# A decoder block on one core: the middle stage gives its last batch to the cross attention, whose maxima then go through one pair of PSUM banks

## The reference

```python
nx = _ln(x, ln1_scale, ln1_bias)
q, k, v = heads(nx @ W_qkv)                       # (4, 16, 1024, 16)
x = x + merge(attend(q, k, v, causal)) @ W_self_out
nx = _ln(x, ln2_scale, ln2_bias)
q = heads(nx @ W_q); k, v = heads(ctx_1024 @ W_kv)   # 154 keys
x = x + merge(attend(q, k, v, None)) @ W_cross_out
nx = _ln(x, ln3_scale, ln3_bias)
return x + relu(nx @ W1 + b1) @ W2 + b2
```

## Time and profile before

| | us |
|---|---|
| median of 3 runs | 997.35 (996.07 to 999.2) |
| profiled execution | 995.61, its span 993.9 |
| TensorE busy | 962.8 (97%) |
| DVE busy | 740.0 (74%) |
| ACT busy | 638.0 (64%) |
| POOL busy | 256.7 (26%) |
| DMA traffic | 124 MB, 38% of the 16 engines' time |

### The profile page before, as it was taken

How to read it: one execution, slowest core, us unless ns; L and a number is a source line. 1 busy time by engine, 2 the same in 40 slices (tenths; PEclk the granted TensorE clock), 3 DMA queues, 4 the chain that set the end, 5 groups by cost and what they waited for, 6 DMA issues and landing times.

```text
span 993.9 us, 20076 instructions
## 1 busy us (share of the span) xinstructions
PE 962.8 (97%) x7632; PEld 605.5 (61%) x7632; DVE 740.0 (74%) x1175; ACT 638.0 (64%) x1371; POOL 256.7 (26%) x451
## 2 busy tenths in 40 slices
PE   4999999999999999999999998999999999999998
PEld 3877664555555555555543764444444699999997
DVE  7578879999999999999923776888887744455542
ACT  4653357777777777777777324788887644444443
POOL 6521122333322222232244110111115212222210
PEclk9999999999999999999999998999999999999999
DMA  7996762222323131313525887244441112221001
GB/s 211 315 349 231 249 193 79 84 93 67 110 66 109 55 102 51 107 51 101 172 85 172 266 318 233 83 136 136 147 129 35 63 45 64 64 65 63 23 23 43
DMA packets 78272, 124.01 MB, mean 125 GB/s; under 512 B 10624, under 2 KB 51872, under 8 KB 73120
## 3 DMA queue, kind: packets, MB, share of 16 engines
q1 hardware_dynamic: 78176, 122.73, 37.8%
HBM read 72.48 MB, written 49.17 MB: 122 GB/s over the span
## 4 chain that ended last, share of the span: by engine, by line
PE 86%; DVE 9%; DMA 2%; issue 1%; ACT 1%; SPq 1%; POOL 0%; ACTq 0%; DVEq 0%
PE bank L862 20%; PE bank L841 18%; PE bank L717 11%; PE bank L698 10%; PE bank L699 9%; PE bank L700 9%; DVE mx L1222 6%; PE bank L725 2%; PE bank L896 2%; PE bank L690 2%; PE bank L685 2%; PE bank L738 1%; DMA qx_parts<-probs 1%; DVE nx_mem L1208 1%; DMA q_st<-qx_parts 1%
## 5 line engine op out<-in xcount | busy, mean ns | idle before, releaser
L1115 ACT ACTIVATE probs<-bank 128x512 f32<-128x512 f32 (+3 forms) x1024 | 455.1, 524 | 122.1 <-PE bank L841 117.2
L1222 DVE TENSOR_REDUCE mx<-bank 128x2 f32<-128x1024 f32 (+5 forms) x416 | 433.6, 1082 | 39.1 <-PE bank L717 27.3
L841 PE MATMUL bank<-q_st,k_st 64*128 64x512 f32 (+3 forms) x1024 | 287.6, 428 | 6.4 <-ACT probs L1115 3.3
L841 PEld LDWEIGHTS bank<-q_st,k_st 64*128 64x128 f32 x1024 | 135.8, 185 | 181.3 <-ACT probs L1115 165.4
L862 PE MATMUL bank<-probs,nx_mem 128*32 128x512 f32 (+3 forms) x2048 | 231.6, 529 | 0.4 <-POOL probs L1583 0.4
L717 PE MATMUL bank<-k_st,q_st 62*128 62x154 f32 (+4 forms) x1280 | 225.7, 348 | 4.9 <-DVE mx L1222 2.6
L717 PEld LDWEIGHTS bank<-k_st,q_st 62*128 62x128 f32 x1280 | 143.5, 187 | 49.2 <-DVE mx L1222 30.5
L1583 POOL TENSOR_SCALAR_AFFINE_SELECT probs<-probs 128x256 f32<-128x256 f32 x256 | 103.9, 407 | 204.8 <-ACT probs L1115 204.2
L1592 POOL TENSOR_TENSOR oN<-oT,rs 128x256 f32<-128x256 f32 x64 | 40.5, 633 | 213.3 <-DVE rs L1326 213.3
L1153 ACT ACTIVATE hT<-bank,b_sb 128x512 f32<-128x512 f32 x64 | 44.2, 690 | 73.0 <-PE bank L700 73.0
L1474 DVE TENSOR_TENSOR hT_lo<-hT,hT_hi 128x512 fp32r<-128x512 f32 x64 | 42.6, 686 | 54.5 <-ACT hT_hi L1156 53.5
(11 more groups left out here) (126 smaller groups left out, 1276.2 us busy)
## 6 DMA issues: line engine op xcount, KB each, us to landing
q_st<-q_parts SPq DMA_DIRECT2D x48, 256.0 KB
q_st<-qx_parts SPq DMA_DIRECT2D x48, 256.0 KB
xt<-in_x_dram SPq DMA_DIRECT2D x16, 512.0 KB, 5.7
q_parts<-probs SPq DMA_DIRECT2D x16, 512.0 KB, 4.3
k_parts<-probs SPq DMA_DIRECT2D x16, 512.0 KB, 4.3
k_st<-k_parts SPq DMA_DIRECT2D x32, 256.0 KB
qx_parts<-probs SPq DMA_DIRECT2D x16, 512.0 KB, 6.3
v_aug<-vst_mem SPq DMA_DIRECT2D x8, 544.0 KB, 4.5
```

Of the source, the lines that this page charges most:

```text
L841: pe.matmul(bank[:, score_bank(a, use), 0:n], keys_of(a, v0)[rows, i // 2, P * kb:P * kb + P], q_st[w][rows, i // 2, lo:lo + n], start=Tru ...
L1115: act.activation(probs[:, use % NPT, 0:n], bank[:, score_bank(a, use), 0:n], ACT.Exp, scale=SCALE).then_inc(a.exp_done, 1)
L1222: dve.tensor_reduce(mx[:, par, part].rearrange("p (j y) -> p j y", j=2)[:, :, blocks.start:blocks[-1] + 1:blocks.step], banks[:, :, 0:len( ...
```

## The change

The last batch (n = 6 and 7) leaves the middle stage. Its two halves are worked off in spans 0 to 8 of cross attention (`late_c` on TensorE, ACT and DVE, `first_e` on SyncE): projection in steps 1 and 2 of a half, transposes in step 10, query products in steps 13 and 14, where a half has 16 steps, that is four spans. They use banks 6 and 7, so the maxima of cross attention have the pair (2, 3) alone from the first tile of span 0 until the turn of span 8 (`RING_X`, `ring_of`). The tiles of units 0 and 1 move to n = 3, 4 and 5. Normalized tokens and product parts of the late batch lie in memory that is free by then (`nx_late`, `parts_late`). SyncE waits for the stored parts of a batch ahead of the loads of its first unit, and loads and stores of the last batch move. For the last two units the ring of score banks begins with the usual ones. In self attention the slots of tiles and sums change. The final stage's first transposes come one step later. The diff, cut to its core:

```diff
         SA = Attention("S", True, L, L // P, q_parts, k_parts, v_aug, self_ctx, [0, 1, 2], [3], [(4, 5), (6, 7)],
-                       units_at=(1, 7, 7, 13, 13, 17, 21, 23, 28, 30, 34, 34, 38, 38, 44, 45, 47, 49, 52, 54), turn_at=2,
-                       weigh_at=(4, 0, 1, 1, 2, 1, 1, 1, 1, 1, 0, 2),
+                       units_at=(1, 7, 7, 13, 13, 18, 22, 24, 29, 30, 34, 34, 37, 40, 43, 43, 46, 49, 53, 53), turn_at=2,
+                       weigh_at=(4, 0, 1, 1, 3, 2, 2, 2, 1, 1, 0, 2),
...
-        EARLY_X = {3: (3,), 4: (1, 3), 5: (1, 3), 6: (0, 1, 2, 3), 7: (0, 1, 2)}
-        LATE_X = 6
+        NC, HALF_STEPS = 2 * B - 2, 16
+        EARLY_X = {3: (3,), 4: (0, 1, 2, 3, 3), 5: (0, 1, 1, 2, 3, 3)}
+        LATE_X = 4
...
-        def ring_x(n):
-            return 1 if n < LATE_X else 2
+        RING_X = (sum(n < LATE_X for n, _ in places_x), 2 * XA.MT + 1, (XA.MT + 1) * (2 * HALF_STEPS // XA.NS + 2) - XA.M0 + 2)
+        def ring_of(a, use):
+            return 1 if a is XA and (use < RING_X[0] or RING_X[1] <= use < RING_X[2]) else 2
...
-            return [y, *(a.s_banks[(use - at + c) % a.SB] for c in range(a.SB)), x][at % END_RING[a]]
+            return [*(a.s_banks[(use - at + c) % a.SB] for c in range(a.SB)), y, x][at % END_RING[a]]
...
@@ SyncE
+                        if a is XA and (v0 + 3) % 4 == 0:
+                            for s in range(4):
+                                sp.wait_ge(C.parts_stored[s], 16 + 16 * ((v0 + 3) // 4 + 1))
                         load_stacks(a, v0 + 3, b, "qk" if a.causal else "q")
...
-            sums_c(2, 0, True)
+            sums_c(2, 0, False)
...
             for hf in range(2):
-                sums_c(3, hf, False)
-                products_c(2, hf)
-                if hf:
-                    keys_x(3)
-                    load_stacks(XA, 2, 0, "q")
-            products_c(3, 0)
+                load_dense(C, x, self_ctx, 3, hf)
+            products_c(2, 0)
+            keys_x(3)
+            load_stacks(XA, 2, 0, "q")
             rows(XA, 0, 0)
-            products_c(3, 1)
             sp.wait_ge(v_spare, 2)
             load_values(XA, 1, 0)
+            products_c(2, 1)
             load_stacks(XA, 3, 0, "q")
...
             def first_e(w):
+                hf, part = divmod(w, HALF_STEPS // XA.NS)
+                if hf < 2 and part == 2:
+                    sums_c(B - 1, hf, False)
+                if 0 < hf < 3 and part == 0:
+                    products_c(B - 1, hf - 1)
...
@@ TensorE
-                    if use == 4 * a.NS * (4 * B - 2):
+                    if use == 4 * a.NS * (4 * B - 2) + a.SB:
                         pe.wait_ge(a.m_free, (a.MT + 1) * 4 * B - 1)
...
+            def late_c(hf, r):
+                n = NC + hf
+                if hf > 1:
+                    return
+                if r in (1, 2):
+                    if hf:
+                        pe.wait_ge(C.lo_ready, 2 + 2 * (n - 1) + r)
+                    elif r == 1:
+                        pe.wait_ge(XA.m_free, RING_X[1])
+                    project_c(B - 1, hf, r - 1, o_bank=6)
+                if r == 10:
+                    transposes(C, n, hf, 6, nx_late)
+                if r in (13, 14):
+                    c = r - 13
+                    pe.wait_ge(C.nxT_ready, 2 * n + 2)
+                    project(bank[:, 6 + c], wqx_sb, slice(P * c, P * c + P), nxT[:, hf]).then_inc(C.p_ready, 1)
...
-                if step == 4:
+                if step == 5:
                     transposes(E, 0, 0, 2)
...
@@ ACT
+                if r == 11:
+                    scaled(C, 1, n, hf, 6)
+                if r in (14, 15):
+                    c = r - 14
+                    if hf:
+                        act.wait_ge(C.parts_stored[c], 16 + 16 * B)
+                    high(C, 2 * n + c, late_part(n, c)[:, 0, :], bank[:, 6 + c, :])
...
@@ DVE, called in window(v0) ahead of each tile n
+            def late_c(hf, w, n):
+                x = NC + hf
+                if w == 0 and n == 0 and 0 < hf < 3:
+                    low(C, 2 * (x - 1) + 1, late_part(x - 1, 1), bank[:, 7, :])
+                if hf > 1:
+                    return
+                if w == 1 and n in (0, 2):
+                    if n == 0:
+                        dve.wait_ge(x1_stored[hf], 16 * (B - 1) + 16)
+                    residual(C, B - 1, hf, n // 2, 6, 32)
+                if w == 1 and n == 3:
+                    moments(C, xn, x, hf)
+                if w == 2 and n == 1:
...
+                    normalize(C, xn, x, hf, nx_late)
+                if w == 3 and n == XA.MT:
+                    low(C, 2 * x, late_part(x, 0), bank[:, 6, :])
```

More of the change, by code:

```diff
@@ L679, in _, with transposes @@
         def _(pe):
-            def transposes(ph, n, hf, b0):
+            def transposes(ph, n, hf, b0, src=None):
                 pe.wait_ge(ph.nx_ready, n + 1)
+                src = nx[:, hf] if src is None else src
                 for k in range(KC):
                     for t in range(TT):
-                        last = pe.transpose(bank[:, b0 + k, P * t:P * t + P], nx[:, hf, t, P * k:P * k + P], ident[:, :])
+                        last = pe.transpose(bank[:, b0 + k, P * t:P * t + P], src[:, t, P * k:P * k + P], ident[:, :])
                     last.then_inc(ph.tp_ready, 1)
@@ L701, in product, with max_tile @@
                 return last
-            def max_tile(a, v0, b, n, ring):
+            def max_tile(a, v0, b, n):
                 v, w = v0 + 4 * b, v0 % 4
                 blocks, k0, keys, _ = a.tiles[n]
-                use, banks = a.tile_use(v, n), unit_banks(a, a.tile_use(v0, n), ring)
+                use, banks = a.tile_use(v, n), unit_banks(a, a.tile_use(v0, n))
+                ring = ring_of(a, use)
+                if a is XA and use == RING_X[2]:
+                    pe.wait_ge(C.lo_ready, 2 + 2 * 2 * B)
                 if n == 0:
@@ L895, in project_c @@
                     for k in range(KC):
-                        last = pe.matmul(bank[:, 4 + i, D * t:D * t + D], cT[:, hf, k, P * (2 * i + t):P * (2 * i + t) + P],
+                        last = pe.matmul(bank[:, o_bank + i, D * t:D * t + D], cT[:, hf, k, P * (2 * i + t):P * (2 * i + t) + P],
                                          wso_sb[:, k, :], start=(k == 0), stop=(k == KC - 1))
@@ L905, in ahead_c @@
                     pe.wait_ge(w_late, 16 * 4)
-                if step % 2 and step < 16:
+                if step % 2 and 0 < step < 16:
                     project_c(0, step // 8, step // 4 % 2, (step // 2 % 2,))
@@ L1116, in slot @@
                                        scale=SCALE).then_inc(a.exp_done, 1)
-                    ahead(q - (4 * B - 2) * a.NS)
+                    ahead(*divmod(q, HALF_STEPS))
                 sequence(act, a, slot)
             act.wait_ge(A.lo_ready, 10 + 10 * B)
-            attention(SA, lambda step: None)
-            for b in range(B):
+            attention(SA, lambda hf, r: None)
+            for b in range(B - 1):
                 for hf in range(2):
@@ L1142, in scaled_e, with late_c @@
                     act.copy(nT_hi[:, hf, k, :], nxT[:, hf, k, :]).then_inc(nxT_high, 1)
-            attention(XA, lambda step: None)
+            def late_c(hf, r):
+                n = NC + hf
+                if hf > 1:
[7 more added lines that the diff above has]
+                    high(C, 2 * n + c, late_part(n, c)[:, 0, :], bank[:, 6 + c, :])
+            attention(XA, late_c)
             def dense_e(b, more):
@@ L1662, in ahead_e @@
                     pool.tensor_tensor(cT_lo[:, hf, k], cT[:, hf, k], cT_hi[:, hf, k].bitcast(F32), ALU.subtract).then_inc(c_lo, 1)
+                hf, r = divmod(step + (4 * B - 2) * XA.NS, HALF_STEPS)
+                if hf < 2 and r == 6:
+                    deviation(C, NC + hf, hf)
                 if step == 2:
```

113 lines of the change are left out of this document (64 added, 49 removed).

## The result

The changed kernel takes **1039.35 us** (median of four runs, 1032.97 to 1047.85) against 996.71 for the kernel before (995.11 to 999.2), a ratio of 1.0432 [1.038 to 1.0484]. The forecast was 1025, in a range of 1009 to 1043. A run more than 1.5% above the fastest of its kernel is left out of a ratio. The profiled execution took 1038.06 us, its span 1036.3 (before 995.61 and 993.9).

The account below looks back on a forecast made before the run. TensorE, nearly fully busy in the middle stage and cross attention, was taken as the bound. -12.7 + 15.5 + 2.3 + 0.5 + 20.4 + 4.6 - 3.0 = +27.6 us on the median 997.35 gave 1025, range 1009 to 1043.

Parts of the forecast that it names:

- rival A: TensorE's clock swings in the one-pair spans, at 1.2 GHz half of 120 us: +15, so 1040 us; chance 0.15.
- the prediction's own signs: First score about 599; spans 0 to 7 13 to 16 us, 11 to 13 10.1; span 10 wait 4 to 5.
- signs of being wrong: Spans under 12.5 us in the eight, a clock row near 0.5 over 10 us there, self attention units under 25 us.
- Step 3: One maxima bank pair in spans 0 to 7: TensorE waits for DVE's reductions inside and between spans, +20.4 us after cover.
- Rival B: Only waits inside the span show, those between are hidden, unit 12's loads come in time: 1010 us; chance 0.10.
- Step 2: Last batch's work inside spans 0 to 8: TensorE +15.5 us, DVE's delayed reductions +2.3, ACT's delayed exponentials +0.5.
- The cover of 3.8 us: In spans 0, 3, 4 and 7 late work between second and third tile hides 0.95 us of wait each.
- Rival D: All new waits are covered by the late work, 15.5 us of it against 20.4 of waits: 1005 us; chance 0.06.
- Step 1: Middle stage without its last batch: first cross attention score at 598.9 instead of 611.6, ended by the row, -12.7 us.
- Step 4: Span 9: unit 12's loads wait for late stores behind an output store, delaying unit 10's row: +4.6 us.
- Step 5: Self attention's order -1, score rings for the last two units and earlier final-stage transposes the rest: -3.0 us together.
- The clock, the step that failed: TensorE's clock falls at 534 and 616 were left at their cost, with no extra loss in the new spans.

Follow-up runs that it names:

- experiment 4: Kernel before with one maxima bank pair in spans 0 to 7, plus useless matmuls in the waits of spans 1 to 7: 1021.65 us, ratio 1.0258.
- experiment 7: Changed kernel with the stores of the last half's query products issued before the output store of window 8: 1033.9 us, ratio 1.0368.
- experiment 6: Changed kernel with DVE's short last reduction of a cross attention span ahead of turning the sums, and the turning back moved: 1032.48 us, ratio 1.0357.
- experiment 10: Kernel before with self attention's new order, the ends, the new cross attention unit places and the first row issued earlier: 990.72 us, ratio 0.9944.
- experiment 11: The kernel of experiment 10 with eight useless matmuls at the start of cross attention: 988.42 us, ratio 0.9913.
- experiment 3: Kernel before, middle stage keeping all batches, with one maxima bank pair in cross attention spans 0 to 7: 1040.94 us, ratio 1.0461.
- experiment 8: Changed kernel with unit 2's query load issued ahead of unit 3's key loads: four runs between 1029.95 and 1047.08 us.

## Why the prediction was right, and where it was not

The sign, the parts and the places were right; the time lay 14 us above the forecast, inside the range, because rival A came on top of the waits, with a price near the one worked out for it. The four sizes behind the rest of the sum were off by +1.9, +3.3, -2.1 and -2.3 us and nearly cancel, which is partly luck.

Of the prediction's own signs, spans 11 to 13 (10.3 us in the mean, forecast 10.1), self attention units above 25 us and the 2 to 3 us of waits a span came out. The first score came at 595.5, not 599; the eight spans took 14.4 to 19.4 us, not 13 to 16; the wait at span 10 was 1.8 us, not 4 to 5. And one of its signs of being wrong, a clock row near 0.5 for more than 10 us, was there: 13.7 us from 687.4.

Part by part, in the profiled executions. The eight spans are split by experiments 4 and 7, set to an equal clock by 0.38 us for each us at the lower level:

| step | forecast | measured |
|---|---|---|
| 1, middle stage | -12.7 | -10.8 |
| 2, late work in the spans, less its cover | +18.3 - 3.8 | +18.1 |
| 3, one pair, without cover | +24.2 | +23.9 |
| 4, load of unit 12 | +4.6 | +2.5 |
| 5, self attention's order, and the ends | -3.0 | -3.7 - 1.6 |
| the clock in the eight spans | 0 | +11.6 |
| the clock elsewhere (a fall less at 534, one more at 756) | 0 | -1.0 + 2.6 |
| the rest (start of self attention, first score to turn, span 8) | 0 | +0.8 |
| sum | +27.6 | +42.4 |

- **Step 3 by the filled kernel.** Eight spans at 109.05 us, set from their 10.2 us of lower clock to the 6.8 us that the kernel before has there: 109.05 - 3.4 x 0.38 = 107.8, against 83.84: +23.9. The forecast was 8 x 1.68 + 10.8 = 24.2. Both kinds of wait stand in the rows, and experiment 6 shows the cause of the second. Rival B is out.
- **Step 2 by difference.** Experiment 7's eight spans took 130.27 us with 18.5 at the lower level; set to 6.8 that is 125.8, so 42.0 more than before, and 18.1 of it is not the pair's. That is what the late work was to cost (15.5 + 2.3 + 0.5) with no cover at all. The cover of 3.8 us by pieces between two tiles does not show; whether it failed or another piece cost that much more was not separated. Rival D, that late work covers the waits, is out.
- **Step 1, the wrong last wait.** The forecast let the row end the stage, and named only unit 1's stack as something that could come late, by 1.5 us. Unit 2's stack was last: tile at 594.75, with the row landed. The size was off by 1.9 us, and the time before it is measured against is itself known to about 1 us: the unchanged stage took 64.6 to 65.3 us in the other kernels.
- **Step 4** was right in its mechanism (stores behind the output store, landing, loads, row; experiment 7) and too dear: from the end of the stores' issue (745.65) to the loads (749.17) it was 3.5 us, not 4.3, and the score that needs the row starts 1.55 us after the row's issue, not 2.5. The profile shows 5.1 us more from span 9's start to the last turn, but 2.6 of them are the clock's, so 2.5 are the queue's.
- **Step 5** was too timid: the order gives 3.7 us, not 1. The middle stage starts 5.4 us sooner: these 3.7, 0.3 by which self attention itself starts sooner, and 1.3 between the last turn and the stage (46.3 us for 47.7). Of the 1.3 the ends are 0.4, and 1.0 is a fall of the clock that this execution lacks: with the same instructions there, it is 46.4 us in experiment 10, whose profile has no fall there, and 47.3 in experiment 11, whose profile has one. At the other end the ends gave 1.2.
- **The clock, the step that failed.** The forecast left the cost of the two falls where it was, since waits of 0.8 and 1.1 us at 756 and 769 had not lowered the clock. In the new spans such waits come several times in every 14 us. Here is the longest fall, after (687.4 to 701.1), and a short one ahead of it:

```profile
676.00:679.00 3.00, 1.35 (x15) 0.77 (x11) 2.73 (x6) 1.61 (x4) 0.62 (x1) 1.00 0.03 12
679.00:682.00 3.00, 3.00 (x20) 0.81 (x21) 1.39 (x3) 1.68 (x4) 0.00 (x0) 0.76 1.03 376
...
685.00:688.00 3.00, 1.54 (x12) 0.91 (x12) 3.00 (x6) 1.92 (x4) 0.62 (x1) 0.89 0.26 70
688.00:691.00 3.00, 3.00 (x18) 0.90 (x16) 2.33 (x8) 1.08 (x2) 1.21 (x2) 0.50 0.40 140
691.00:694.00 3.00, 3.00 (x17) 1.47 (x17) 1.12 (x1) 1.68 (x3) 0.00 (x0) 0.50 0.00 0
```

TensorE was busy 1.35 and 1.54 us of 3 just ahead, then ran at 0.76 and 0.50, fully busy, the same work taking longer. Rival A had 60 us at the lower level for 15 us; the changed kernel's four runs have 35 to 73, and 42 us more than before in the profile (at 0.39, 16 us). Its chance of 0.15 was the misjudgement. The evidence against it was two single waits in a busy stretch; the evidence for it, in the same rows, was that the fall at 616 followed a window with 1.87 us busy of 3, and the stretch forecast was to be idle more than any other. (The fall at 534 has no idle of its own ahead of it in the profile, only scores whose groups of four took 1.48 and 1.68 us, at 530.84 and 532.60, where 0.73 is usual.) Experiments 3 and 4 are what shows it: the same waits filled with useless work cost 19.3 us less.
The rule quoted from the Trainium skill (TensorE: Matmul & The Clock Gate, "A second HAM failure mode: psum-queue depth-cycling"), that short idles between groups of matmuls in a cycle through PSUM banks can make the clock swing, is what these spans do, and this case's runs agree with it: 58.6 us at the lower level with the waits open, 10.2 with them filled.

**Left open.** Which waits bring the clock down is not settled. In experiment 3's windows TensorE had only 38.88 of 50 us of work between 650 and 700 and a clock of 0.99, and 0.67 in the 50 us before. So where the falls come is not fixed by the waits alone; it differs from run to run of one kernel, and its runs spread over 15 us where the kernel before spreads over 4. Whether the cover in step 2 failed is open too.

## What to carry to other kernels

Moving work from one full stage to another is worth only what the first stage's waits give back; price the buffers it needs there: one bank pair less cost 24 us here and the work itself 18, for 11 us won. A loop that waits for another engine on each round has a second price on TensorE, the clock: on this kernel 0.38 us for each us at the lower level, and the waits' sum of 24 us drew 12 us more behind it. Where such waits can't be removed, useless matmuls that fit inside them, into a bank that is free at the time, cost nothing in experiment 4 and mostly kept the clock. An order that shortens one wait can move others: price it in every stretch where it holds (experiment 6 won in eight spans and lost in the later ones). And where a transfer is late, look first at what its queue issues ahead of it.

## What the runs showed of the hardware

- More matmuls, less time: 84 useless matmuls, 512 columns each, took a kernel from 1040.94 to 1021.65 us. Eight took another from 990.72 to 988.42, with intervals that overlap a little.
- The difference between executions of one program can be the clock alone: spans of 1031.2 to 1046.1 us lie within 1.5 us of one line over the time at 1.2 GHz. Not every idle stretch brings a fall: one window of 50 us had 38.88 us of TensorE's work and a clock of 0.99.
- Where the DMA engines were nearly full, a load issued 5.4 us sooner came only 3.0 us sooner (experiment 8).
